# Adaptive layer norm, linear attention and a mixture of experts on one core: scores by halves of 32 keys, wide weight sets, and scatters placed one by one

## The reference, cut to what matters

```python
h = _layernorm(x, axis=-1) * (1 + ca) + sa
x = x + ga * _L0_attn_ref(h, L0_attn_w_attn, L0_attn_w_proj)
h = _layernorm(x, axis=-1) * (1 + cb) + sb
x = x + gb * _L0_ffn_ref(h, L0_ffn_W1, L0_ffn_W2, L0_ffn_Wg, L0_ffn_bg)

# attention: q, k = elu(.) + 1, per head, causal and linear
def step(carry, qkv_t):
    S, z = carry
    qt, kt, vt = qkv_t
    S = S + kt[..., :, None] * vt[..., None, :]
    z = z + kt
    num = jnp.einsum('bhi,bhij->bhj', qt, S)
    den = jnp.sum(qt * z, axis=-1, keepdims=True)
    return ((S, z), num / (den + EPS))

# experts: each token goes to the expert with the largest logit
logits = xf @ Wg + bg
one_hot = jax.nn.one_hot(jnp.argmax(logits, axis=-1), e, dtype=x.dtype)
h = jax.nn.gelu(jnp.einsum('td,edh->eth', xf, W1), approximate=True)
y = jnp.einsum('eth,ehd->etd', h, W2)
out = jnp.einsum('etd,te->td', y, one_hot)
```

## Time and profile before

| | us |
|---|---|
| median of 3 runs (lowest, highest) | 336.8 (335.36, 338.79) |
| the profiled execution | 336.95 |
| its span, first to last instruction | 335.2 |
| PE busy | 266.8 |
| DVE busy | 219.9 |
| ACT busy | 158.0 |
| POOL busy | 151.8 |

### The profile page before, as it was taken

One profiled execution on the slowest core, in us unless ns is written; L12 is line 12 of the kernel. 1 busy time (PEld: TensorE's weight loads), 2 busy tenths in 40 slices (PEclk: granted clock), 3 DMA queues, 4 the chain that ended last, 5 costly groups with the idle time before them and its releaser, 6 DMA issues.

```text
span 335.2 us, 13040 instructions
## 1 busy us (share of the span) xinstructions
PE 266.8 (80%) x5095; PEld 221.5 (66%) x5095; DVE 219.9 (66%) x780; ACT 158.0 (47%) x317; POOL 151.8 (45%) x173
## 2 busy tenths in 40 slices
PE   0564898988798798699699879775949689999990
PEld 0333777676476576567557657664849689999990
DVE  4985539688579478568568768768665645455540
ACT  3059595534345146146065264004525347777740
POOL 8939600352560570471453355330354734455552
PEclk9957899999799899989979999979978959999996
DMA  7990000000100200200200110111673634444410
GB/s 212 336 304 4 0 5 4 3 5 28 72 4 5 98 2 4 98 2 4 91 9 4 57 44 4 55 47 48 182 209 111 231 107 128 128 125 143 132 41 0
DMA packets 17461, 25.85 MB, mean 77 GB/s; under 512 B 2747, under 2 KB 13117, under 8 KB 17410
## 3 DMA queue, kind: packets, MB, share of 16 engines
q1 hardware_dynamic: 13616, 16.12, 16.9%
q0 software_dynamic: 3360, 8.73, 7.3%
q10 hardware_dynamic: 434, 0.27, 0.4%
HBM read 14.78 MB, written 10.78 MB: 76 GB/s over the span
## 4 chain that ended last, share of the span: by engine, by line
PE 52%; DVE 24%; issue 11%; another core or an unknown queue 4%; ACT 4%; DMA 1%; POOL 1%; SPq 1%; POOLq 0%; DVEq 0%; ACTq 0%
PE bank L1176 11%; PE bank L1321 11%; PE bank L1330 10%; DVE probs L750 5%; PE bank L1129 4%; DVE z_t L815 3%; PE bank L1211 2%; DVE row_buf L808 2%; PE bank L1225 2%; DVE row_buf L806 2%; PE bank L1131 2%; DVE mean L660 2%; PE bank L1162 2%; PE bank L1314 1%
## 5 line engine op out<-in xcount | busy, mean ns | idle before, releaser
L1176 PE MATMUL bank<-q_m,k_q 128*64 128x128 f32 x1024 | 72.3, 285 | 9.1 <-DVE probs L750 5.7
L1176 PEld LDWEIGHTS bank<-q_m,k_q 128*64 128x64 f32 x1024 | 56.6, 140 | 18.8 <-DVE probs L750 9.3
L750 DVE TENSOR_TENSOR probs<-bank,causal 128x256 f32<-128x256 f32 x128 | 51.5, 420 | 25.9 <-PE bank L1176 16.5
L411 POOL DMA_INDIRECT sorted_rows<-row_buf,slot_i x32 | 31.6, 988 | 65.5 <-DVE slot_i L875 57.2
L446 POOL DMA_INDIRECT out_dram<-q_m,slot_token x39 | 38.9, 997 | 38.5 <-DVE q_m L1038 25.8
L1321 PE MATMUL bank<-q_m,k_q 128*128 128x128 f32 x312 | 44.0, 287 | 7.4 <-issue 7.4
L1321 PEld LDWEIGHTS bank<-q_m,k_q 128*128 128x128 f32 x312 | 40.4, 203 | 7.9 <-issue 7.9
L1330 PE MATMUL bank<-k_q,v_m 128*128 128x128 f32 x312 | 43.0, 283 | 1.1 <-issue 1.1
L1330 PEld LDWEIGHTS bank<-k_q,v_m 128*128 128x128 f32 x312 | 39.8, 200 | 1.5 <-issue 1.3
L1211 PE MATMUL bank<-probs,v_m 128*32 128x64 f32 x1024 | 21.9, 225 | 16.7 <-DVE probs L750 16.3
L391 POOL TENSOR_TENSOR guess<-var,minus_half 128x4 f32<-128x4 f32 x8 | 8.3, 1039 | 54.2 <-DVE var L663 54.2
(11 more groups left out here) (208 smaller groups left out, 493.4 us busy)
## 6 DMA issues: line engine op xcount, KB each, us to landing
v_m<-sorted_rows SPq DMA_DIRECT2D x23, 196.0 KB, 2.3
...
out_dram<-q_m,slot_token POOLq DMA_INDIRECT x39
sorted_rows<-row_buf,slot_i POOLq DMA_INDIRECT x32
```

Source lines behind the costliest of these rows:

```text
L411: pool.indirect_dma_start(sorted_rows, bass.IndirectOffsetOnAxis(ap=slot_i[par][:, t:t + 1], axis=0), row_buf[par][:, t, :], None).then_in ...
L750: V.tensor_tensor(probs[:, s, b, q, :], score_bank[q % 2][:, 0:QUADS * L], causal[:].rearrange("p a t -> p (a t)"), ALU.mult).then_inc(pro ...
L1176: last = mm(score_bank[q % 2][L * half:L * half + L, 2 * L * n:2 * L * n + 2 * L], k_q[par][:, q, tok:tok + L], q_m[par][:, 2 * half:2 * h ...
```

## The change

1. **Scores by halves of keys.** The 64 keys of a chunk are split in two halves of 32. The first half meets all 64 queries, the second only queries 32 to 63, so each of the 2 x 2 products per chunk has 32 weight columns and 128 or 64 moving columns. In odd chunks the two halves of keys swap their partitions. A part is now FIRST = 0 (quads 0 and 1, bank S0) or LAST = 1 (quads 2 and 3, bank S1); a bank holds both quads, 512 elements, and DVE masks it by one operation. `probs_ready` and `score_mm` count parts instead of quads.
2. **Rows of v, k_t and the mask follow.** In odd chunks `front_qkv` and `front_kt` write the two halves of 32 tokens to swapped partitions, by four products with 32 weight columns instead of two with 64. The mask `causal` is made by four selects on 32 partitions instead of two on 64.
3. **Wide weight sets.** den, logits and ranks use 128 weight columns: 4, 4 and 2 products instead of 16, 16 and 8.
4. **POOL's order.** Group r - 1's four scatters stand singly in round r: behind the root, behind the norm, between the halves of k_q and behind them. The last two groups' scatters are put among the row writes of the first slots.

The core of the diff:

```diff
-FIRST, LAST = (0, 1), (2, 3)
+FIRST, LAST = 0, 1
...
-        causal = sb("causal", [P, QUADS, L])
+        causal = sb("causal", [P, 2, 2, L])
...
             for half in range(2):
-                rows = slice(L * half, L * half + L)
-                nc.gpsimd.affine_select(out=causal[rows], in_=causal[rows], compare_op=ALU.is_ge, fill=0.0, base=0,
-                                        pattern=[[0, QUADS], [1, L]], channel_multiplier=-1).then_inc(masks, 1)
+                for part in range(2):
+                    at = L * half + 32 * part
+                    rows = slice(at, at + 32)
+                    last = nc.gpsimd.affine_select(out=causal[rows], in_=causal[rows], compare_op=ALU.is_ge, fill=0.0,
+                                                   base=-32 * part, pattern=[[64 * part - 32, 2], [0, 2], [1, L]],
+                                                   channel_multiplier=-1)
+                    if part == 0:
+                        chain.link(last)
+                last.then_inc(masks, 1)
...
+            def route(r):
+
+
+                par, old = r % 2, 1 - r % 2
                 route_root(r)
+                if r:
+                    route_scatter(r - 1, old, [0])
                 route_norm(r, par)
-                front_kq(r + 2, par)
-                route_scatter(r, par)
...
+                if r:
+                    route_scatter(r - 1, old, [1])
+                if r < G - 2:
+                    front_kq(r + 2, par, (0, 1))
+                if r:
+                    route_scatter(r - 1, old, [2])
+                if r < G - 2:
+                    front_kq(r + 2, par, (2, 3))
+                if r:
+                    route_scatter(r - 1, old, [3])
...
             for n in range(RING * OPEN):
-                if n == SCATTER_AT:
-                    route_scatter(G - 1, 1)
+                if n < 2:
+                    route_scatter(G - 2, 0, [2 + n])
+                if SCATTER_AT <= n < SCATTER_AT + GT:
+                    route_scatter(G - 1, 1, [n - SCATTER_AT])
                 rows_out(n, n % RING)
...
-            def core_probs(g, s, b, quads=range(QUADS)):
+            def core_probs(g, s, b, part):
                 wait_ge(dve, y_mm, 4 * g + 2 * s - 1)
-                for q in quads:
-                    dve.wait_ge(score_mm, 16 * g + 8 * s + 4 * b + q + 1)
-                    V.tensor_tensor(probs[:, s, b, q, :], score_bank[q % 2][:, 0:QUADS * L],
-                                    causal[:].rearrange("p a t -> p (a t)"), ALU.mult).then_inc(probs_ready, 1)
+                dve.wait_ge(score_mm, 8 * g + 4 * s + 2 * b + part + 1)
+                V.tensor_tensor(probs[:, s, b, 2 * part:2 * part + 2, :],
+                                score_bank[part][:].rearrange("p (q t) -> p q t", q=2),
+                                causal[:].rearrange("p n a t -> p (n a t)").unsqueeze(1).broadcast_to(
+                                    [P, 2, QUADS * L]), ALU.mult).then_inc(probs_ready, 1)
...
+            def token_rows(n, half):
+
+                if n % 2 == 0:
+                    return [(slice(L * half, L * half + L), slice(n * L, n * L + L))]
+                return [(slice(L * half + 32 - 32 * part, L * half + 64 - 32 * part),
+                         slice(n * L + 32 * part, n * L + 32 * part + 32)) for part in range(2)]
...
                 for t in range(GT):
-                    for j in range(4):
-                        rows = slice(32 * j, 32 * j + 32)
-                        last = mm(F2[rows, HEADS * t:HEADS * t + HEADS], qz[:, t * P + 32 * j:t * P + 32 * j + 32],
-                                  block[:].rearrange("p (h j) -> p h j", j=HD)[:, :, 0], start=True, stop=True)
+                    last = mm(F2[:, HEADS * t:HEADS * t + HEADS], qz[:, t * P:(t + 1) * P],
+                              block[:].rearrange("p (h j) -> p h j", j=HD)[:, :, 0], start=True, stop=True)
...
-                    pe.wait_ge(probs_ready, 16 * g + 8 * s + 4 * b + q + 1)
+                pe.wait_ge(probs_ready, 8 * g + 4 * s + 2 * b + part + 1)
+                for q in range(2 * part, 2 * part + 2):
                     for n in range(2):
                         tok = t * P + n * L
-                        for half in range(2):
-                            last = mm(score_bank[q % 2][L * half:L * half + L, 2 * L * n:2 * L * n + 2 * L],
-                                      k_q[par][:, q, tok:tok + L], q_m[par][:, 2 * half:2 * half + 2, tok:tok + L],
-                                      start=True, stop=True)
-                    last.then_inc(score_mm, 1)
+                        out_of = score_bank[part][:, 256 * (q % 2) + 128 * n:256 * (q % 2) + 128 * n + 128].rearrange(
+                            "p (a t) -> p a t", a=2)
+                        for keys in (1 - n, n):
+                            for half in range(2):
+                                at = L * half + 32 * (keys ^ n)
+                                last = mm(out_of[at:at + 32, :, 32 * keys:L],
+                                          k_q[par][:, q, tok + 32 * keys:tok + 32 * keys + 32],
+                                          q_m[par][:, 2 * half:2 * half + 2, tok + 32 * keys:tok + L],
+                                          start=True, stop=True)
+                last.then_inc(score_mm, 1)
```

69 lines of the change are left out of this document (31 added, 38 removed).

## The result

| | before | changed | ratio (95% interval) |
|---|---|---|---|
| median of 20 runs each, us | 339.43 | 335.6 | 0.988 (0.983 to 0.992) |
| lowest, highest | 334.76, 341.6 | 330.31, 340.01 | |
| the profiled execution (span) | 336.95 (335.2) | 332.81 (331.0) | |

What follows compares the result with a forecast made beforehand. It took waits between PE and DVE, mainly PE completions held behind rows of scatters, as the bound. 336.95 - 13.2 - 2.4 - 4 - 4.5 + 4 + 1.7 = 318.5 us; own range 312 to 325, whole range 304 to 332.

Steps and rivals of the forecast that it cites:

- If the hold needs a row of them, all five holds go: -13.2: Long attention steps: only back-to-back scatters delay PE's completion signals, so spreading them saves 13.2 us over five steps.
- rival 2: Attention steps: each single scatter delays PE's signals, so the hold returns in pieces; 328 or 338 us, chance 0.07 each.
- The bound of half the holds, 328: Attention steps: half of the 13.2 + 2.4 + 4 us saved on holds comes back, giving 328 us; chance 0.07.
- +0.4 a step on the path: Attention steps: of PE's +1.4 us of work a step, 0.4 lengthens the step; with collisions, +4 us in all.
- mean clock 1.00 there: Attention steps: expected sign that PE runs at full clock in all steps, with steps of about 23 us.
- The wait for the bank: Attention scores: with a bank for each part, scores no longer wait until DVE has read the bank; -4.5 us in all.
- The last step: Last attention step: L1225 to L1211 takes 5.09 us against 2.70 without scatters, so -2.4; -1.8 with other terms.
- The experts: Expert part: idle stretches behind rows of indirect DMAs and the slow clock cost together 12 us; -4 taken.
- Rival 1: Expert part: its holds go as well, because rows of DMAs of different kinds don't hold; 310.5 us, chance 0.20.
- The start: Before the first projection: four mask selects delay POOL's memsets and DVE, +0.9; the first group's PE work +0.8; +1.7 us.
- Rival 3: v, k_t and scores: PE's changes of weight shape make it slower; 356 us, or 337 with holds gone; chance 0.08.
- Rival 4: Expert fetches: later last scatters of groups 5 and 7 use up slack of about 1.3 us; +4, 322 us, chance 0.06.

Runs made afterwards that it cites:

- b_spread: The kernel before with only POOL's order changed, scatters one by one: 320.4 us against 339.1 for the kernel before, chip A.
- a_pieces32: The changed kernel with all chunks of v and k_t by 32 weight columns: 322.3 us against 339.2 for the kernel before, chip B.
- a_placed: The changed kernel with single scatters moved to where nobody waits for a PE signal: 323.1 us against 339.1 for the kernel before, chip A.
- a_tab32: The changed kernel with den, logits and ranks by 32 weight columns again: 326.7 us against 339.2 for the kernel before, chip B.
- a_both32: The changed kernel with narrow den, logits and ranks and uniform 32-wide pieces of v and k_t: 309.7 us, ratio 1.013 to the kernel before, chip C.
- a_fill: The changed kernel with products of zeros ahead of PE's waits: 325.5 us against 339.2 for the kernel before, chip B.
- b_mask4: The kernel before with its mask made by four selects: 304.5 us, ratio 0.994 to the kernel before, chip C.

## Why the prediction was wrong

*The step that failed* is this one: "If the hold needs a row of them, all five holds go: -13.2." The hold needs no row. Single scatters have it, which was rival 2 (0.14 in all): where the kernel before takes 339 us, at most one signal of PE in a whole trace comes between 0.7 and 1.34 us behind one of the 20. In the kernel before, with its scatters spread, the single holds meet next to nothing that anybody needs (b_spread, -13.2 us in the long steps as forecast). The term came out to the tenth there because single holds are shorter than those of a row and meet little, and not because they are gone. In the changed kernel the fourth meets the last scores of a step (0.94 us of waiting), and the second cuts within 1 (0.44). The five steps came out at -0.1 where -13.8 were forecast. The bound of half the holds, 328, was too kind, because I had no price for the clock behind them.

*"+0.4 a step on the path"* failed with it. The products themselves cost what I had worked out, or less. These are their rows, in the step of 79.05:

```profile
84.82 2.13 PE L1162 MATMUL bank<-wqkv,h_t 128*64 128x64 f32 x48
...
87.35 1.53 PE L1207 MATMUL bank<-q_m,k_q 128*32 128x64 f32 x64
...
99.79 1.06 PE L1179 MATMUL bank<-block,qz 128*128 128x16 f32 x8 [0.59 <-DVE qz L852]
```

v takes 0.98 us more than the earlier trace rows's k_t group of the same shape (forecast 7 x 0.14 = 0.98) and den 0.61 more (forecast 0.6). One part of scores alone takes 0.87 and two take 1.53, so a further part adds 0.66, where before it was 8 rounds of 0.12, 0.96: 0.3 saved a part (forecast 0.17). Step 1, where no scatter is, came out at -0.7 against -0.3. What I missed is where this work puts PE's signals. v and k_t stand ahead of the last scores and, with the 0.44 us of the second hold, move them from 14.1 to 15.4 us into a step, while the fourth scatter stays at 15.9 to 16.0: the scores now end behind its start. a_pieces32 and a_placed bear this out, each from its side, and a_tab32, which takes away work behind the meeting, leaves it. A second cause is argued only: a bank with both quads gives DVE one signal where it had two, so that one held signal stops it altogether. The run meant to separate the two (a_both32: scores by halves, but narrow sets and uniform pieces) came onto a chip without held signals. And of the 2.1 us that a long step takes over step 1, a_placed gave back 1.0; the rest stays open.

*The half clock* was no term of mine but "mean clock 1.00 there". The clock fell behind waits of 0.97 and 0.91 us in the steps from 129.46 and 183.75, and 10 us of it cost 3.8 us in the first of these. The other three long steps have the same wait and keep the full clock, so the wait alone does not decide it. a_fill prices the half clock at 6 us in the long steps.

*The wait for the bank* (-4.5) is gone, as forecast: no row of the changed kernel has scores waiting for DVE. What that is worth alone no run shows; it is part of the 0.7 us of step 1.

*The last step* (-1.8 forecast, +0.5 measured): PE waits 3.52 us for the modulated rows and then works at half clock. POOL's scatter between root and norm is not the reason: b_spread has it too, and its last step takes 18.21 us at full clock.

```profile
219.23 1.03 POOL L404 TENSOR_TENSOR row_buf<-row_buf,mean 128x512 f32<-128x512 f32 x1 [0.84 <-DVE rstd L687]
...
222.95 0.95 PE L1266 MATMUL bank<-ident,row_buf 128*128 128x128 f32 x4 [3.52 <-DVE row_buf L826]
```

The rows come 11.7 us into the step, in b_spread 11.2 (213.51); PE is ready for them sooner, and its clock falls. With a_fill's 14 products of zeros ahead of this wait the step takes 19.65 us.

*The experts* (-4 forecast, -1.1 measured): the idle stretch of 4.56 us of the earlier trace rows is gone, but ones of 0.7, 0.8, 2.0 and 2.2 us remain, and 5 us of the half clock that began before 223.4 lie in this part. Rival 1, that these holds go as well, did not happen; on chip C (b_mask4) this part takes 12.6 us less.

*The start* (+1.7 forecast, -2.8 measured): I had read rightly that DVE is held by the memsets, and then moved the end of the hold with them by 0.9 us. It did not occur to me that the shift could let DVE through before the second pair.

*Rival 3*, the changes of weight shape, is half right: they cost what it said per product, and a_pieces32 wins 13.3 us by taking them away, but on chip D the long steps of the kernel that has them (118.4 us) are no longer than those of the one that has not (118.8). *Rival 4*, late data, played no part: in the experts of the changed kernel no wait of PE is put down to a DMA.
